# Four layers of a graph network in one kernel: in layer 0, squares, sums, norms and low halves issued later than what they need

## The chip, the cores and the metric

One Trainium2 chip, one of its cores. The metric is the device time of one execution in microseconds; the kernel before takes 1052.36 us (median of three runs, 1052.09 to 1052.92).

## The reference, cut to what matters

`x` is 8 x 2048 x 64, `adj` 2048 x 2048 (a 0/1 matrix with under 1% ones, rows divided by their sums). Four layers follow, each of the form `x = layernorm(x + f(x))`, the layer norm being over the 64 channels:

```python
# layer 0, K = 3, D = 16
w = einsum('nd,dkio->nkio', embedding, weight); b = embedding @ bias
As = [I, A, 2 A A - I]
out = einsum('bnki,nkio->bno', einsum('knm,bmc->bnkc', stack(As), x), w) + b
# layer 1: attention whose mask adj > 0.5 is nearly empty; in effect a mean over the rows, then elu
# layer 2: ((adj + I) @ (x W^T + b)) / rowsum;  layer 3: three steps of v = relu([v, adj v] W1 + b1) W2 + b2
```

## The kernel before, in words

**Layout.** Batch and channel are one axis of 512, cut into four chunks c of 128 columns (two batch entries). The 2048 nodes are 16 tiles of 128; four tiles make a part j. A pair (c, j) is a unit, u = 4c + j. The 0/1 matrix lies in SBUF in fp8, values in pairs of fp16 halves: a high half by ScalarE out of PSUM (`act_e1`, `act_e2`, `act_dx`: L1017, L1023, L1032) and a low half, the rest, by VectorE out of the same PSUM bank (`lo_half`, recorded as L1203). A bank is free for the next user when its low half is done.

**Layer 0.** Per unit a product P1 (A x) and a product P2 (A A x), each four quarters of 8 matmuls (`quarter`, L750), then per node tile t a round Z (L880): 36 matmuls against the 16 weight matrices, in two halves g of 18 matmuls, each into a pair of banks. For each half VectorE takes five of the eight results d with one operation each, multiplied with the embedding's column and added onto `X` or `Y` (L1203, the first `Y` L1195), ScalarE takes the other three (L1043, tiles `AT`), and GpSimd adds them up (`add`: a 128x384, two 128x128, two more onto X). ScalarE starts a half only after VectorE's last operation of it (`s_acc`), and after GpSimd's first operation of the add before (`s_ab`). TensorE may start half n when ScalarE has done half n - 2 (`s_za`).

There are 64 rounds, (u,t) or in one number 4u+t. Between rounds the order puts quarters of P1 (units 2, 3 of each chunk) and of P2 (the next unit, always bank 0), and in the first two units of chunks 0 to 2 after even rounds `dx` (L725, L726) and after odd rounds `t1` (L788, L789), of the next chunk. dx, t1 and the mean (L886) all use the one bank 1 (`pe_aux` waits until its last user is read out). GpSimd makes t1's low half (L1708).

**Layers 0 and 1 behind the rounds.** Each chunk c, when its 16 rounds are done, gets its layer norm: squares of each part (`sq`, ScalarE), their sum by VectorE (L1206, in the same step), a variance (`var`), a square root on ScalarE, a root refined in five small VectorE operations (`rs`, L1495 to L1499), and `apply` (L1505). Then `sum` over the parts (GpSimd, three 128x512 additions), `mean` (two fp32 matmuls against ones), `row_a`, `row_b` (VectorE and ScalarE, small), `addrow` onto X (GpSimd), squares and norm again (L = 1), and `split` into fp16 halves for layer 2 (ScalarE, GpSimd, and an addition by GpSimd). `scales` 0, 1, 2 are chains of small VectorE operations on scale factors, with two `hat` halves; they are needed in the tail.

**The order** is written by hand. `HEAD` (L84) is the list up to the first round, `middle_order` (L95) lays steps at places `(u, t)` of the rounds, and what falls behind the last round is given to `last_order` (L149), which writes the tail: products P(k) of layers 2 and 3 with evacuation E(k), and the rest beside them. Every engine walks the same list and takes its own part of each step (`tensor_steps`, `scalar_steps`, `vector_steps`, `gpsimd_steps`), in that order. The squares of layers 0 and 1 have one buffer, `SQ` in `T3`. In a round the list is:

```python
            order += [("Z", u, t), ("add", u, t)]
            order += after.pop((u, t), [])
            if c < 3 and j < 2:
                v = 4 * (c + 1) + 2 * j + t // 2
                order.append(("dx" if t % 2 == 0 else "t1", v))
```

`dve_xs` and `pool_xs` centre two tiles of x each and add the bias (`xs` 0 to 7); `bounds` ends with a GpSimd all-reduce over the partitions (L1741).

Of the kernel before, what the change touches and what calls it, by code (L numbers as in the profile page):

```python
# [14 lines left out]
NT = 16  # L15
# [65 lines left out]
def place(p, c, j):  # L81
# [9 lines left out]
        + [("xs", 0), ("xs", 1)]  # L91
        + pieces("P1", 2) + [("t1", 2), ("dx", 3), ("t1", 3), ("E1", 10), ("bounds",), ("xs", 2)]
# [3 lines left out]
def middle_order():  # L96

    after = {}
# [22 lines left out]
    order = []  # L121
    for k in range(5):
        at(k // 2, 1 + 2 * (k % 2), ("xs", 3 + k))
    at(2, 3, ("scales", 0))
    at(3, 1, ("scales", 1))
    at(3, 2, ("scales", 2))
    for u in range(16):
# [17 lines left out]
        order += after.pop((u, 4), [])  # L145
    return order, after


def last_order(after):  # L149
# [8 lines left out]
    for (u, t) in sorted(after):  # L158
        at(u - 16, *after[u, t])
    for c in range(NC):  # L160
        for j in range(4):
            at(4 * c + j + 3, ("W", c, j))
            at(4 * c + j + 4, ("sq", 2, c, j))
# [70 lines left out]
    between[55] = [("F", *x), ("sq", 3, *v), ("var3", *u)]  # L234
    on(56, ("root3", *u), ("rs3", *u), *outs(7, 5), ("F", *y), ("sq", 3, *x), ("sq", 3, *y), ("var3", *x), ("root3", *x),
# [38 lines left out]
def gnn_kernel(nc, x_in, at_in, a_in, embt_in, sm_in, bx_in, w0_in, a12_in, w0bb_in, out):  # L274
    ctx = ExitStack()
    with ctx:
# [147 lines left out]
        SQ = [T3[:, 512:1024]]  # L424
# [200 lines left out]
        SQN, SQPREV, VARN, RSN = {}, {}, {}, {}  # L625
# [5 lines left out]
        def number_norms():  # L631
            held = {}
            for x in MIDDLE + TAIL:
                if x[0] == "sq":
                    buf = 0 if x[1] < 2 else 2 * x[1] - 3 + len([y for y in SQN if y[0] == x[1]]) % 2
                    SQPREV[x[1:]] = held.get(buf)
                    SQN[x[1:]] = len(SQN)
                    held[buf] = x[1:]
                elif x[0] in ("var", "root3"):
# [6 lines left out]
        REDN = {x: n for n, x in enumerate(y for y in SQN if y[0] < 3 or order3(*y[1:]) > 12)}  # L646
# [14 lines left out]
        def sq_buf(L, c, j):  # L661
            return SQ[0] if L < 2 else SQC[2 * L - 4 + [y for y in SQN if y[0] == L].index((L, c, j)) % 2]
# [183 lines left out]
        def tensor_steps(e, steps):  # L846
            for step in steps:
# [9 lines left out]
                elif kind == "Z":  # L857
                    u, t = step[1:]
                    c, j = divmod(u, 4)
                    n4 = 4 * u + t  # L860
# [6 lines left out]
                    for g in range(2):  # L867
                        n = 2 * n4 + g
                        b0 = z_bank(n)
                        if n < 3:  # L870
                            for b in (b0, b0 + 1):
                                e.wait_ge(*z_first[b])
                        else:
                            e.wait_ge(s_za, 3 * (n - 2))
                        for i in range(9):
                            kd, part = divmod(i, 3)
                            zh, wh = ((0, 0), (0, 1), (1, 0))[part]
                            for q in range(2):
                                r = slice(64 * q, 64 * q + 64)
                                m = e.matmul(bank(b0 + q), halves[kd][zh][r, :], WZ[r, wh, kd, block(g)],  # L880
                                             start=(i == 0), stop=(i == 8))
                        m.then_inc(s_zp, 1)
# [158 lines left out]
        def scalar_steps(e, steps):  # L1041
# [3 lines left out]
            for step in steps:  # L1045
# [9 lines left out]
                elif kind == "scales" and step[1] == 0:  # L1055
# [5 lines left out]
                elif kind == "Z":  # L1061
                    u, t = step[1:]
# [4 lines left out]
                    for g in range(2):  # L1067
                        e.wait_ge(s_acc[0], 5 * n4 + (3, 5)[g])
                        e.wait_ge(s_acc[1], 5 * n4 + (2, 5)[g])
                        ps = zpair(2 * n4 + g)  # L1070
                        for d in range(DV, 8):
                            fn(grid(AT[:, 3 * g + d - DV, :]), ps[:, :, d, :], ACT.Copy,
                               scale=emb[:, it, 8 * g + d:8 * g + d + 1]).then_inc(s_za, 1)
# [291 lines left out]
        def vector_steps(e, steps, fc):  # L1365
# [31 lines left out]
            def scales_c():  # L1397
# [7 lines left out]
                for t in range(2):  # L1405
                    e.wait_ge(s_hh, 2 + t)
# [864 lines left out]
```

## Time and profile before

| | |
|---|---|
| median of 3 runs | 1052.36 us (1052.09 to 1052.92) |
| the profiled execution | 1052.66 us, its span 1050.9 us |
| TensorE matmul busy | 1023.4 us, 97% |
| TensorE clock granted | 0.996 of full |
| VectorE, ScalarE, GpSimd busy | 690.4, 453.4, 538.1 us |
| DMA | 45.66 MB, 43 GB/s on average, nearly all before 60 us and after 510 us |

The span runs from the first to the last instruction of the program. The head (loads, first products) lasts to about 103 us, the rounds of layer 0 from 110 to 531, the tail from there on. PE is TensorE, DVE VectorE, ACT ScalarE, POOL GpSimd. Idle times before an instruction stand in brackets behind it with who ended them.

### The profile page before, as it was taken

The page shows a single profiled execution, that of the slowest core. Times are in us where ns is not written, and L with a number is a line of the kernel's source. Part 1 is how long each engine was busy: PE and PEld are TensorE (multiplying, and loading weights), DVE is VectorE, ACT ScalarE, POOL GpSimd, SP SyncE. Part 2 cuts the span into 40 slices and gives each one's busy share as a digit, 9 for nine tenths or more (in the row PEclk, how much of TensorE's full clock was granted, in tenths as well). Part 3 has the DMA queues.
Part 4 walks back from the last instruction along what each step waited for, and adds up shares of the span by engine and source line. Part 5 has one row for each costly group of instructions (what it writes and reads, how often), then busy time and mean ns, then how long its engine had stood idle before and what let it go on. Part 6 is the DMA issues. An engine that isn't in the chain of part 4 may idle for free.

```text
span 1050.9 us, 18768 instructions
## 1 busy us (share of the span) xinstructions
PE 1023.4 (97%) x6922; PEld 490.9 (47%) x6922; DVE 690.4 (66%) x1728; ACT 453.4 (43%) x1097; POOL 538.1 (51%) x625
## 2 busy tenths in 40 slices
PE   7999999999999999999999999999999999999995
PEld 3445444434443444344345555555554545455553
DVE  3876565677547765775674778876546677767556
ACT  4632333333334343534423677557556622132632
POOL 0005486546456766775671757579764232223311
PEclk9999999999999999999999999999999999999998
DMA  9930000000000000000010121212112100000022
GB/s 365 400 128 1 2 1 2 1 2 1 1 1 2 1 1 2 1 1 2 1 41 1 41 81 41 81 41 80 53 69 81 41 1 1 3 2 21 22 61 61
DMA packets 14658, 45.66 MB, mean 43 GB/s; under 512 B 960, under 2 KB 9280, under 8 KB 10080
## 3 DMA queue, kind: packets, MB, share of 16 engines
q1 hardware_dynamic: 14560, 44.39, 11.4%
q8 instruction: 57, 0.93, 0.4%
q14 instruction: 41, 0.34, 0.1%
HBM read 40.19 MB, written 4.19 MB: 42 GB/s over the span
## 4 chain that ended last, share of the span: by engine, by line
PE 84%; DVE 9%; POOL 2%; ACT 2%; DMA 2%; issue 1%; SPq 0%; POOLq 0%; ACTq 0%; DVEq 0%
PE PS L750 34%; PE PS L880 21%; PE PS L924 18%; DMA BW<-at_in 2%; PE PS L735 2%; PE PS L737 2%; PE PS L736 2%; DVE BW L1200 1%; DVE T L1203 1%; DVE X L1203 1%; PE PS L744 1%; PE PS L742 1%; PE PS L743 1%; ACT T L1043 1%; PE PS L725 1%
## 5 line engine op out<-in xcount | busy, mean ns | idle before, releaser
L750 PE MATMUL PS<-BW,S 128*128 128x512 fp8e4 x1792 | 403.5, 379 | 4.3 <-POOL S L1708 1.9
L750 PEld LDWEIGHTS PS<-BW,S 128*128 128x128 f16 x1792 | 169.6, 98 | 211.0 <-issue 15.9
L1043 ACT ACTIVATE T<-PS,SM 128x128 f32<-128x128 f32 x384 | 112.5, 365 | 206.9 <-DVE X L1203 137.7
L880 PE MATMUL PS<-WZ,R 64*128 64x512 f16 x1536 | 198.5, 377 | 3.1 <-ACT T L1043 3.1
L1745 POOL TENSOR_TENSOR T<-T 128x128 f32<-128x128 f32 (+1 forms) x192 | 127.0, 662 | 124.9 <-ACT T L1043 114.4
L1203 DVE SCALAR_TENSOR_TENSOR X<-PS,SM,X 128x128 f32<-128x128 f32 x320 | 109.9, 344 | 38.7 <-PE PS L880 38.5
L880 PEld LDWEIGHTS PS<-WZ,R 64*128 64x128 f16 x1536 | 69.2, 94 | 106.8 <-issue 25.4
L924 PE MATMUL PS<-BW,S 128*128 128x512 fp8e4 x512 | 115.4, 379 | 0.4 <-issue 0.4
L1745 POOL TENSOR_TENSOR S<-R,S 128x512 f16<-128x512 f32 x48 | 57.5, 1210 | 94.2 <-ACT S L1043 94.2
L880 PE MATMUL PS<-WZ,T 64*128 64x512 f16 x768 | 103.8, 376 | 0.0
L1203 DVE SCALAR_TENSOR_TENSOR T<-PS,SM,T 128x128 f32<-128x128 f32 x256 | 88.0, 344 | 21.2 <-PE PS L880 21.2
L1745 POOL TENSOR_TENSOR T<-R,T 128x512 f16<-128x512 f32 x42 | 49.6, 1187 | 74.7 <-DVE T L1195 52.7
L1767 POOL TENSOR_TENSOR BW<-BW 128x512 fp8e4<-128x512 fp8e4 x64 | 75.6, 1208 | 0.0
L1043 ACT ACTIVATE R<-PS,cs 128x512 f32<-128x512 f32 x48 | 32.7, 681 | 98.7 <-PE PS L744 68.7
L924 PEld LDWEIGHTS PS<-BW,S 128*128 128x128 f16 x512 | 49.1, 98 | 55.9 <-issue 0.9
L924 PE MATMUL PS<-BW,T 128*128 128x512 fp8e4 x320 | 72.8, 379 | 0.0
L1745 POOL TENSOR_TENSOR X<-X,T 128x128 f32<-128x128 f32 x128 | 59.4, 464 | 10.0
L1043 ACT ACTIVATE WZ<-WZ,ra 128x2048 f16<-128x2048 f32 (+1 forms) x32 | 63.9, 1996 | 0.5
L1195 DVE TENSOR_SCALAR T<-R 128x512 f16<-128x512 f32 x48 | 31.5, 657 | 47.5 <-ACT R L1043 46.6
L802 PE MATMUL PS<-BW,S 128*128 128x512 fp8e4 x240 | 53.6, 386 | 6.0 <-DVE BW L1200 6.0
L735 PE MATMUL PS<-hat,T 128*128 128x128 f16 x320 | 56.8, 219 | 2.4 <-DVE T L1203 2.4
L880 PEld LDWEIGHTS PS<-WZ,T 64*128 64x128 f16 x768 | 37.4, 94 | 45.5
(215 smaller groups left out, 1476.9 us busy)
## 6 DMA issues: line engine op xcount, KB each, us to landing
WZ<-a_in SPq DMA_DIRECT2D x16, 1024.0 KB, 4.8
BW<-at_in SPq DMA_DIRECT2D x8, 1024.0 KB, 18.3
R<-at_in SPq DMA_DIRECT2D x7, 1024.0 KB, 13.7
out<-X SPq DMA_DIRECT2D x16, 256.0 KB, 2.3
X<-x_in SPq DMA_DIRECT2D x3, 1024.0 KB, 20.3
T<-w_in SPq DMA_DIRECT2D x1, 1536.0 KB, 16.0
R<-at_in SPq DMA_DIRECT2D x2, 512.0 KB, 5.2
SM<-sm_in SPq DMA_DIRECT2D x1, 520.5 KB, 18.3
```

What stands on the lines that cost most here:

```text
L735: e.matmul(ok, th, hat[:, 0, kind, :], start=True, stop=False)
L736: e.matmul(ok, tl, hat[:, 0, kind, :], start=False, stop=False)
L737: m = e.matmul(ok, th, hat[:, 1, kind, :], start=False, stop=True)
L750: m = e.matmul(o, stile(h, t, c), Bm[:, t, block(j)], start=(t == 0 and h == 0), stop=(last and t == NT - 1 and h == 1))
L802: e.matmul(bank(2 * c + j), stile(h, jt, c), Bm[:, jt, block(j)], start=(jt == 0 and h == 0), stop=False)
L880: m = e.matmul(bank(b0 + q), halves[kd][zh][r, :], WZ[r, wh, kd, block(g)], start=(i == 0), stop=(i == 8))
L924: m = e.matmul(o, half_of(n, what, h, q % 2)[:, t, :], b[:, 4 * (q % 2) + t, :], start=(s in (0, 1, 3) and q % 2 == 0 and t == 0 and h == ...
L1043: return e.activation(o, i, f, **kw)
L1195: return e.tensor_scalar(o, i, s1, None, o1)
L1203: return e.scalar_tensor_tensor(out=o, in0=a, scalar=s, in1=b, op0=f, op1=g)
L1745: return e.tensor_tensor(o, a, b, f)
L1767: e.tensor_tensor(o, a, b, f, saturate=False).then_inc(s_bt, 1)
```

## The change

Steps are laid at a round number g = 4u + t instead of (u, t), later and more spread than before. In chunks 0 to 2, with g the chunk's end: squares 2 or 3 rounds behind their unit's last round, their sum (a step of its own, `red`) a round behind the square; `var` at g+3, `rs` at g+4, one `apply` a round, `sum` at g+7, `mean` at g+9, `row_b` at g+10, `addrow` at g+11 to g+14, squares two rounds behind it, `var` at g+17, `apply` and `split` one a round from g+18. Chunk 3, whose steps mostly fall in the tail, has a denser list of its own. The low halves of P1's and P2's evacuations and of dx leave their step and go between VectorE's two halves of the next Z. Z is two steps (g = 0, 1). The first piece of `scales` is in two, the hat halves are steps of their own, and the long pieces go behind the first product of the tail. The squares get four buffers in the part of `BW` that later holds `BT`. In the head the second `xs` goes behind t1 2 and 3.

```diff
-        + [("xs", 0), ("xs", 1)]
-        + pieces("P1", 2) + [("t1", 2), ("dx", 3), ("t1", 3), ("E1", 10), ("bounds",), ("xs", 2)]
+        + [("xs", 0)]
+        + pieces("P1", 2) + [("t1", 2), ("dx", 3), ("t1", 3), ("xs", 1), ("E1", 10), ("bounds",), ("xs", 2)]
...
-    def at(u, t, *steps):
-        after.setdefault((u, t), []).extend(steps)
+    after, rest = {}, {}
+    def at(g, *steps):
+        (after if g < 64 else rest).setdefault(g if g < 64 else g - 64, []).extend(steps)
 
     for c in range(NC):
+        g = 16 * c
         for j in range(4):
-            at(4 * c + j + 1, 1, ("sq", 0, c, j))
-        u = 4 * c + 4
-        at(u, 2, ("var", 0, c))
-        at(u, 3, ("rs", 0, c), ("apply", 0, c, 0), ("apply", 0, c, 1))
-        at(u, 4, ("apply", 0, c, 2), ("apply", 0, c, 3), ("sum", c))
-        if c == 3:
-            u += 4
-        at(u + 1, 1, ("mean", c), ("row_a", c))
-        at(u + 1, 3, ("row_b", c))
-        for j in range(4):
-            at(u + 2, j, ("addrow", c, j))
-            at(u + 2, j + 1, ("sq", 1, c, j))
-        at(u + 3, 0, ("var", 1, c))
-        at(u + 3, 1, ("rs", 1, c), ("apply", 1, c, 0), ("split", c, 0))
-        for j in (1, 2, 3):
-            at(u + 3, j + 1, ("apply", 1, c, j), ("split", c, j))
+            late = (c, j) == (3, 3)
+            at(g + 4 * j + (5 if late else 6), ("sq", 0, c, j))
+            at(g + 4 * j + (6 if late else 7), ("red", 0, c, j))
+        g += 16
+        if c < 3:
+            at(g + 3, ("var", 0, c))
+            at(g + 4, ("rs", 0, c), ("apply", 0, c, 0))
+            for j in (1, 2, 3):
+                at(g + 4 + j, ("apply", 0, c, j))
+            at(g + 7, ("sum", c))
+            g += 9
+            at(g, ("mean", c), ("row_a", c))
+            at(g + 1, ("row_b", c))
+            for j in range(4):
+                at(g + 2 + j, ("addrow", c, j))
+                at(g + 4 + j, ("sq", 1, c, j))
+                at(g + 5 + j, ("red", 1, c, j))
+            at(g + 8, ("var", 1, c))
+            for j in range(4):
+                at(g + 9 + j, *[("rs", 1, c)][j:], ("apply", 1, c, j), ("split", c, j))
+        else:
+            at(g + 2, ("var", 0, c))
+            at(g + 3, ("rs", 0, c), ("apply", 0, c, 0), ("apply", 0, c, 1))
+            at(g + 4, ("apply", 0, c, 2), ("apply", 0, c, 3), ("sum", c))
+            at(g + 6, ("mean", c), ("row_a", c))
+            at(g + 7, ("row_b", c))
+            for j in range(4):
+                at(g + 7 + j // 3, ("addrow", c, j))
+                at(g + 8 + j // 3, ("sq", 1, c, j))
+                at(g + 9, ("red", 1, c, j))
+            at(g + 9, ("var", 1, c))
+            for j in range(4):
+                at(g + 10 + j // 2, *[("rs", 1, c)][j:], ("apply", 1, c, j), ("split", c, j))
     for k in range(5):
-        at(k // 2, 1 + 2 * (k % 2), ("xs", 3 + k))
-    at(2, 3, ("scales", 0))
-    at(3, 1, ("scales", 1))
-    at(3, 2, ("scales", 2))
+        at(2 * k + 1, ("xs", 3 + k))
+    at(9, ("scales", 0))
+    at(11, ("scales", 1))
+    at(13, ("scales", 2))
+    at(15, ("scales", 3))
+    at(65, ("scales", 4), ("scales", 5))
+    order, lo = [], []
...
                 order.append(beside.pop(0))
-            order += [("Z", u, t), ("add", u, t)]
-            order += after.pop((u, t), [])
+                if order[-1][0][0] == "E":
+                    lo.append(("lo", *order[-1]))
+            order += [("Z", u, t, 0), *lo, ("Z", u, t, 1), ("add", u, t)]
+            lo = []
+            order += after.pop(4 * u + t, [])
             if c < 3 and j < 2:
                 v = 4 * (c + 1) + 2 * j + t // 2
                 order.append(("dx" if t % 2 == 0 else "t1", v))
+                if t % 2 == 0:
+                    lo.append(("lo", *order[-1]))
...
-        SQ = [T3[:, 512:1024]]
+        SQ = [BW[:, NT * N + 2048 * k:NT * N + 2048 * k + 2048].bitcast(F32) for k in range(4)]
...
-                elif kind == "sq":
-                    L, c, j = step[1:]
-                    if L == 3 and summed_by_act(c, j):
-                        continue
+                elif kind == "red":
+                    L, c, j = step[1:]
                     o = st_part(L, c, j, 0)
                     e.wait_ge(s_sq, SQN[L, c, j] + 1)
                     red(e, o if L == 3 else o[:, 8 * j:8 * j + 8], grid(sq_buf(L, c, j)), ALU.add).then_inc(s_red, 1)
```

The tail's own lists get a `red` beside each `sq` whose sum VectorE makes, at the same place; the buffers of its squares stay.

## Rows read from the trace of the kernel before

**Rows 1.** The page, part 4: the chain that ended last, by engine.
```profile
PE 84%; DVE 9%; POOL 2%; ACT 2%; DMA 2%; issue 1%; SPq 0%; POOLq 0%; ACTq 0%; DVEq 0%
```

**Rows 2.** Timeline of TensorE, round (6,3): start us, us, engine, line, operation.
```profile
306.62 0.82 PE L880 MATMUL PS<-WZ,R 64*128 64x512 f16 x6
...
310.61 1.90 PE L750 MATMUL PS<-BW,S 128*128 128x512 fp8e4 x8
```

**Rows 3.** Timeline of TensorE: the longer rounds, and a mean without a wait.
```profile
214.88 0.82 PE L880 MATMUL PS<-WZ,R 64*128 64x512 f16 x6
...
221.20 1.90 PE L750 MATMUL PS<-BW,S 128*128 128x512 fp8e4 x8 [1.80 <-DVE R L1203]
...
257.83 0.82 PE L880 MATMUL PS<-WZ,R 64*128 64x512 f16 x6
...
263.97 0.23 PE L788 MATMUL PS<-i,T 128*128 128x128 f16 x1 [1.03 <-DVE ROW L1206]
...
264.43 3.62 PE L750 MATMUL PS<-BW,S 128*128 128x512 fp8e4 x16
...
368.25 0.82 PE L880 MATMUL PS<-WZ,R 64*128 64x512 f16 x6
...
374.99 0.23 PE L788 MATMUL PS<-i,T 128*128 128x128 f16 x1 [1.62 <-DVE ROW L1206]
...
418.93 0.82 PE L880 MATMUL PS<-WZ,R 64*128 64x512 f16 x6
...
421.98 0.82 PE L880 MATMUL PS<-WZ,R 64*128 64x512 f16 x6 [0.94 <-ACT T L1043]
...
424.03 1.90 PE L750 MATMUL PS<-BW,S 128*128 128x512 fp8e4 x8
...
470.73 1.13 PE L886 MATMUL PS<-SM,ones 128*128 128x512 f32 x2
471.70 1.89 PE L750 MATMUL PS<-BW,S 128*128 128x512 fp8e4 x8
```

**Rows 4.** The chain in order of time: one product of the tail.
```profile
547.03 6.91 PE PS L750 x32
```

**Rows 5.** Timelines of TensorE, GpSimd and ScalarE around the head's end.
```profile
103.13 7.08 PE L750 MATMUL PS<-BW,S 128*128 128x512 fp8e4 x32 [1.93 <-POOL S L1708]
...
123.98 1.46 PE L880 MATMUL PS<-WZ,R 64*128 64x512 f16 x12
...
117.83 1.03 POOL L1717 TENSOR_TENSOR X<-X,hat 128x512 f32<-128x512 f32 x1 [6.93 <-issue]
...
123.54 1.66 ACT L1043 ACTIVATE T<-PS,SM 128x128 f32<-128x128 f32 x6 [6.45 <-POOL T L1745]
```

**Rows 6.** Timelines of VectorE, TensorE: Z, a low half, who waits.
```profile
116.41 0.82 PE L880 MATMUL PS<-WZ,R 64*128 64x512 f16 x6
...
118.64 0.35 DVE L1203 SCALAR_TENSOR_TENSOR X<-PS,SM,X 128x128 f32<-128x128 f32 x1 [0.82 <-PE PS L880]
...
308.78 0.35 DVE L1203 SCALAR_TENSOR_TENSOR X<-PS,SM,X 128x128 f32<-128x128 f32 x1 [0.73 <-PE PS L880]
...
309.82 0.34 DVE L1203 SCALAR_TENSOR_TENSOR X<-PS,SM,X 128x128 f32<-128x128 f32 x1
...
334.32 0.69 DVE L1203 SCALAR_TENSOR_TENSOR R<-PS,R 128x512 f16<-128x512 f32 x1 [1.42 <-ACT R L1023]
334.93 0.34 DVE L1203 SCALAR_TENSOR_TENSOR X<-PS,SM,X 128x128 f32<-128x128 f32 x1
...
335.07 1.25 PE L750 MATMUL PS<-BW,S 128*128 128x512 fp8e4 x5
```

**Rows 7.** Applies (ns min/median/max), one root with its apply.
```profile
L1505 DVE TENSOR_TENSOR X<-X,T x28: 682/904/1758, 248.5 to 546.1; 128x512 f32<-128x512 f32 x28
...
324.78 0.34 DVE L1495 RECIPROCAL T<-T 128x32 f32<-128x32 f32 x1
...
327.07 0.69 DVE L1505 TENSOR_TENSOR X<-X,T 128x512 f32<-128x512 f32 x1
```

More of the change, by code:

```diff
@@ L144, in middle_order @@
                 order.append(("dx" if t % 2 == 0 else "t1", v))
-        order += after.pop((u, 4), [])
-    return order, after
+                if t % 2 == 0:
+                    lo.append(("lo", *order[-1]))
+    return order, rest
 def last_order(after):
@@ L156, in at @@
         late.setdefault(k, []).extend(steps)
-    for (u, t) in sorted(after):
-        at(u - 16, *after[u, t])
+    for k in sorted(after):
+        at(k, *after[k])
     for c in range(NC):
@@ L661, in sq_buf @@
         def sq_buf(L, c, j):
-            return SQ[0] if L < 2 else SQC[2 * L - 4 + [y for y in SQN if y[0] == L].index((L, c, j)) % 2]
+            return (SQ + SQC)[SQBUF[L, c, j]]
         def st_part(L, c, j, k, m=1):
@@ L866, in tensor_steps @@
                               [U2[:, u % 3, h, 128 * t:128 * t + 128] for h in range(2)])
[L867 to L882, printed above, removed]
+                    n = 2 * (4 * u + t) + g
+                    b0 = z_bank(n)
+                    if n < 3:
+                        for b in (b0, b0 + 1):
+                            e.wait_ge(*z_first[b])
+                    else:
+                        e.wait_ge(s_za, 3 * (n - 2))
+                    for i in range(9):
+                        kd, part = divmod(i, 3)
+                        zh, wh = ((0, 0), (0, 1), (1, 0))[part]
+                        for q in range(2):
+                            r = slice(64 * q, 64 * q + 64)
+                            m = e.matmul(bank(b0 + q), halves[kd][zh][r, :], WZ[r, wh, kd, block(g)],
+                                         start=(i == 0), stop=(i == 8))
+                    m.then_inc(s_zp, 1)
                 elif kind == "mean":
@@ L1054, in scalar_steps @@
                     act_e2(e, step[1])
-                elif kind == "scales" and step[1] == 0:
+                elif kind == "scales" and step[1] == 1:
                     e.wait_ge(s_xc, NT)
@@ L1066, in scalar_steps @@
                         e.wait_ge(s_ab, n4)
[L1067 to L1073, printed above, removed]
+                    e.wait_ge(s_acc[0], 5 * n4 + (3, 5)[g])
+                    e.wait_ge(s_acc[1], 5 * n4 + (2, 5)[g])
+                    ps = zpair(2 * n4 + g)
+                    for d in range(DV, 8):
+                        fn(grid(AT[:, 3 * g + d - DV, :]), ps[:, :, d, :], ACT.Copy,
+                           scale=emb[:, it, 8 * g + d:8 * g + d + 1]).then_inc(s_za, 1)
                 elif kind == "sq":
@@ L1404, in scales_c @@
                 e.wait_ge(s_sc, 1)
-                for t in range(2):
-                    e.wait_ge(s_hh, 2 + t)
-                    stt(e, hat[:, 1, t:4:2, :], BD[:, t::2, :], cs[:, cRho64 + t:cRho64 + t + 1], hat[:, 0, t:4:2, :],
-                        ALU.mult, ALU.subtract).then_inc(s_hl, 1)
             for step in steps:
                 kind = step[0]
-                if kind == "E1":
-                    dve_e1(e, step[1])
+                if kind == "lo" and step[1] == "E1":
+                    dve_e1(e, step[2])
+                elif kind == "lo" and step[1] == "E2":
+                    dve_e2(e, step[2])
+                elif kind == "lo" and step[1] == "dx":
+                    dve_dx(e, step[2])
+                elif kind == "lo":
+                    e.wait_ge(s_zh, 1)
+                    lo_half(e, T[:, 0, 1, block(0)], bank(product_bank(0)), T[:, 0, 0, block(0)], s_zl)
@@ L1524, in vector_steps @@
                     ts(e, ROW[:, 0, :], ROW[:, 0, :], LAM, None, ALU.mult).then_inc(s_row, 1)
-                elif kind == "E":
+                elif kind == "E" and step[1] > 0:
                     k = step[1]
```

83 lines of the change are left out of this document (42 added, 41 removed).

## The prediction

> **What bounds it now.** The chain that ended last [rows 1] is 84% TensorE, so a part of the kernel off TensorE counts only where it makes TensorE wait. The change touches layer 0 (about 103 to 531 us) and the first products of layer 1 behind it. A busy share says little there: matmuls are drawn 0.38 us long while they start every 0.11 or 0.22 us, so short waits vanish in it. I read the timeline of TensorE, start to start; (u,t) is round t of unit u, number 4u+t. A quiet round (36 matmuls of Z) takes 3.99 us from its first matmul to the first of what follows [rows 2]: 306.62 to 310.61. Every other round is held against that.
>
> The rounds that take longer [rows 3] are these. Round (3,3): 214.88 to 221.20 is 6.32, so 2.33 lost; VectorE was in the scale steps 1 and 2, Z's second half came late and then the product waited for bank 0's low half (1.80 idle). Round (5,1): 257.83 to the t1 at 263.97 is 6.14; the mean's two fp32 matmuls cost 0.97 where nobody waits (470.73 to 471.70), so 1.18 lost, TensorE wanting bank 1 while VectorE had still to reduce the mean. Round (9,1): 368.25 to 374.99, 1.78 lost in the same way. Rounds (7,1), (11,1), (15,1): 418.93 to 424.03 is 5.10, 1.11 lost in each of the three; the wait is for ScalarE's copies (421.98), which stood behind a VectorE that was held by the one buffer of squares and by addrow. Together 2.33 + 1.18 + 1.78 + 3 x 1.11 = 8.6 us, plus some 0.2 in two small waits: **8.8 us** is all that TensorE waits between its first round and the layer's end.
>
> **What the change removes.** The two long scale steps go to the tail's second step, and the hat halves to rounds 13 and 15: the 2.33 go. About 5 us of small VectorE operations land beside the tail's products, where a stage has 32 matmuls of product, 6.91 us, at the least [rows 4], and its low half is wanted two products later: cost nothing; without that cover it would be their 5 us. The means go to rounds 25, 41 and 57, where no dx or t1 follows for bank 1: 1.18 + 1.78 go (the mean's own 0.97 stays). Squares come two rounds behind addrow, with four buffers, and sums a round behind the squares: the 3 x 1.11 go. Nothing is added in instruction count; the squares only change address, and the writer of BT gets to those 8 KB a row late in the tail. For chunk 3, sums, mean and splits come 3 or 4 tail stages later; product 12 wants them at stage 12 and they are issued at 10 and 11, so nothing again. No DMA moves; GpSimd's queue keeps its operations, with sum 4 rounds later.
>
> **The head.** TensorE stands 1.93 us before 103.13 for GpSimd's t1 [rows 5]. With the second xs behind t1 it would come about 2 us sooner. But GpSimd's work to the first add is the same sum in another order: after it comes the all-reduce, and xs 2 begins at 117.83 as before. ScalarE's copies of round 1 wait for the first add and start at 123.54 and are six in 1.66; half of them are done 0.9 later, and the second half of round 2 (the second six of the twelve matmuls at 123.98, so about 124.63) needs it. TensorE can start it at 124.48 at the earliest. Gain 0.15, not 2.
>
> **What the change adds: low halves behind Z's first half.** A low half frees a PSUM bank: bank 0 for the next product, bank 1 for the t1 behind dx. Until now VectorE did it ahead of Z, in idle time. Now it stands behind the five operations of Z's first half. In a quiet round [rows 2, 6] these start at 308.78, 2.16 after the round's start, the fifth at 309.82, so the low half at 310.08, 3.46 in. From a low half's start to the matmul that waits for it: 334.32 to 335.07 is 0.75 (this low half is late already, ahead of (8,0)). So TensorE may go on at 4.20, and could at 3.99: **a stall of 0.21**. In chunk 0 the first operation comes at 2.23 (116.41 to 118.64): 0.28. Where dx's and a product's low halves stand together, the second starts 0.61 later (334.32 to 334.93), that is allowed at 4.81; t1 starts at 4.20 and gives over after 0.46 (263.97 to 264.43): another 0.15.
>
> Counting from the order: ten rounds have a product's low half alone before bank 0 is wanted (chunk 0: three; rounds (6,3), (7,3), (10,3), (11,3), (12,3), (13,3), (14,3); at (6,1) the mean covers it): 3 x 0.28 + 7 x 0.21 = 2.3. Dx alone: (4,1), (8,1), (9,1), 0.6 (the one at (0,1) is swallowed by the wait at 124.5). Both: three in chunk 0, five later: 3 x 0.43 + 5 x 0.36 = 3.1. Sum **6.0 us lost**, in 21 small waits.
>
> **What else makes a low half late.** VectorE is free from about 5.4 us into a round to 2.16 into the next: 2.6 us in short rounds (5.82), 3.0 in those with dx or t1 (6.27). A root (rs, five operations) and one apply took 2.9 (324.78 to 327.07, and 0.61 of the apply's 0.69) [rows 7]. That fits after round 34, is 0.3 over after round 50 (a low half follows), and round 36 has rs and two applies, 0.9 over; with the waits behind them about **1.1 us**. The bounds: nothing, if the pieces are the quick ones; and 5.3 us if every apply is the slowest of its row (1.76) and every root the slow one (2.28): 1.0 + 2.8 + 1.5.
>
> That spread has a cause in the rows: the same apply takes 0.68 to 1.76 [rows 7], and it is the longer ones that stand beside GpSimd's additions; the change puts splits (two GpSimd operations a round) and applies in the same rounds. The Trainium skill says so too (SBUF — State Buffer, on the shared port pair): a VectorE operation with two SBUF inputs and a GpSimd operation exclude each other, the later fully blocked. By that rule the upper bound is the one to fear; by the rows' median of 0.90 it is the middle one. The trace agrees with the rule in kind, its share here is open.
>
> **Sum.** 8.8 + 0.15 - 6.0 - 1.1 = 1.9 us faster. The profiled execution took 1052.66 (span 1050.9), 0.3 above the median of 1052.36; so 1050.8 for it, and **1050.4** as a median. About 0.2% (2.1 us) is what a measurement here can tell from none, and this lies just within it.
>
> **Rivals.**
> 1. *The low halves cost TensorE next to nothing*: bank 0 and 1 come free in time, as they do wherever TensorE arrives late. Then 8.8 + 0.15 - 1.1 = 7.9, 1044.5. For it: 0.2 us on a 4 us round is thin, and half of it gone gives 1047.5. Against: each of the three terms (2.16, 1.30, 0.75) is a plain difference of two rows of a quiet stretch. Chance 0.17.
> 2. *Slower*: VectorE is late with low halves in many rounds, since applies and roots now run beside splits and additions and take their slow lengths. Place: rounds 34 to 37 and 50 to 53, then each low half behind them. Price: 5.3 us by the upper bound above, 8.95 - 6.0 - 5.3 = -2.4, 1054.7. It decides (slower by over 0.2%) from 5.1 us of lateness on. Chance 0.08.
> 3. *The change does not do all that it says*: a removed wait comes back elsewhere, for instance Z's second half still waits for ScalarE in three rounds (3.3 us), since GpSimd's queue has sum, t1 and splits in the way: 1053.7. For it: copies wait for GpSimd's first operation of the add before (6.45 us idle at 123.54). Against: from that operation's usual time to the moment at which it would hurt are 5 us, and sum is 3.8. Chance 0.15.
>
> **Numbers.** Forecast 0.60, its own range 1048.7 to 1052.3. It lies on the bound of faster (1050.26), so it splits: 0.25 faster, 0.35 within. Rival 1 is faster, rival 3 is within but for 0.02, rival 2 is slower. Faster 0.43, same 0.48, slower 0.09. The range goes down half way to rival 1, since a stall of 0.1 in place of 0.2 is the nearest error, and up beyond the forecast toward rival 3: 1046.5 to 1053.2.
>
> **What the profile would show.** TensorE's rounds (3,3), (5,1), (7,1), (9,1), (11,1), (15,1) at 3.99 (4.96 with a mean), or the step is wrong. Quiet rounds with a low half at 4.20 in place of 3.99, and waits of products and t1 on VectorE's low halves: some 21 of 0.2 to 0.4 us. The page's span near 1049. The second half of round 2 still at about 124.5 with the wait on ScalarE. No new wait of TensorE behind layer 0. If the low halves' waits are absent the forecast is wrong by up to 6 us, if there are waits over 0.5 us behind rounds 34 to 53, rival 2 is at work.

## The result and the profile after

The changed kernel takes 1056.1 us (median of 9 runs, 1054.34 to 1057.28) against 1052.8 of the kernel before beside it (9 runs, 1052.09 to 1053.77): ratio 1.003 with the interval 1.002 to 1.0041, so it is slower by 3.3 us. Its profiled execution took 1056.91, that of before 1052.66, so the comparison of the traces has 4.25 us to explain. The prediction was 1050.4 (range 1046.5 to 1053.2): wrong in sign, and outside its range.

The page of the changed kernel: span, engines, and the chain of work that ended last by engine:

```profile
span 1055.1 us, 18890 instructions
...
PE 1027.2 (97%) x6922; PEld 492.1 (47%) x6922; DVE 691.8 (66%) x1728; ACT 452.7 (43%) x1097; POOL 533.6 (51%) x625
...
PE 76%; DVE 14%; issue 3%; ACT 3%; DMA 2%; POOL 2%; SPq 0%; ACTq 0%; DVEq 0%; POOLq 0%
```

TensorE's share of the chain fell from 84% [rows 1] to 76% and VectorE's rose from 9% to 14%: TensorE is waiting for VectorE in more places. Where, the view of TensorE's waits says, here for 100 to 540 us, which is layer 0 (line, releaser: us in total, times, longest):

```profile
PE PS L820 <- DVE R L1232: 3.1, 6, 2.0
PE PS L910 <- ACT T L1073: 1.7, 1, 1.7
PE PS L782 <- DVE R L1232: 1.2, 3, 0.8
...
```

The same view of the changed kernel for 540 to 1040 us:

```profile
PE PS L767 <- DVE R L1232: 1.6, 2, 1.0
PE PS L757 <- DVE X L1232: 1.0, 1, 1.0
...
```

Before, the second stretch had 0.8 us of waits, at 916 and 1036 us, none of them in the tail's first 120 us. As in the prediction, the waits are better read start to start. The two traces laid side by side, the 4.25 us come out as:

| where | us |
|---|---|
| first round starts at 107.75 instead of 110.14 | -2.39 |
| its low half, and round 2, which waits 1.83 in its middle | +2.10 |
| the six long rounds [rows 3] are at 3.99 (the means 0.95 more) | -8.8 |
| low halves behind Z's first half | +6.0 |
| rounds 35, 37 and 51 longer than that (0.14, 1.84, 0.64) | +2.6 |
| TensorE at its lower clock in round 37 | +1.6 |
| three waits in the tail | +3.05 |
| sum (trace: last round +1.12, from there on +3.1) | 4.2 |

**A low half costs what was worked out.** Timeline of TensorE of the changed kernel in round (6,3), the quiet round of [rows 2]:

```profile
306.19 0.82 PE L910 MATMUL PS<-WZ,R 64*128 64x512 f16 x6
...
310.39 0.82 PE L782 MATMUL PS<-BW,S 128*128 128x512 fp8e4 x3
```

And of VectorE beside it, the first operation of Z's first half and the low half behind the fifth:

```profile
308.35 0.35 DVE L1232 SCALAR_TENSOR_TENSOR X<-PS,SM,X 128x128 f32<-128x128 f32 x1 [2.92 <-PE PS L910]
...
309.65 0.68 DVE L1232 SCALAR_TENSOR_TENSOR R<-PS,R 128x512 f16<-128x512 f32 x1
```

306.19 to 310.39 is 4.20 where before had 3.99. The same 0.21 stands in every such round of chunks 1 to 3, 0.27 or 0.28 in chunk 0, and 0.15 more where dx's and a product's low halves stand together.

**Round 37 waits far longer, and then TensorE runs at half clock.** Timeline of VectorE of the changed kernel:

```profile
366.92 1.33 DVE L1537 TENSOR_TENSOR X<-X,T 128x512 f32<-128x512 f32 x1
368.17 0.34 DVE L1527 RECIPROCAL T<-T 128x32 f32<-128x32 f32 x1
368.55 0.77 DVE L1528 TENSOR_TENSOR T<-T 128x32 f32<-128x32 f32 x1
369.35 0.92 DVE L1529 TENSOR_TENSOR T<-T 128x32 f32<-128x32 f32 x1
...
370.51 0.33 DVE L1531 TENSOR_TENSOR T<-T 128x32 f32<-128x32 f32 x1
370.88 0.99 DVE L1537 TENSOR_TENSOR X<-X,T 128x512 f32<-128x512 f32 x1
...
373.09 0.67 DVE L1232 SCALAR_TENSOR_TENSOR R<-PS,R 128x512 f16<-128x512 f32 x1
```

And of TensorE, first matmul of the t1 that waits for it, and the product behind:

```profile
373.82 0.23 PE L820 MATMUL PS<-i,T 128*128 128x128 f16 x1 [1.98 <-DVE R L1232]
...
374.28 3.43 PE L782 MATMUL PS<-BW,S 128*128 128x512 fp8e4 x8
```

From 366.92 to 371.87 VectorE has two applies and a root between two rounds of Z, 4.95 us where such a round leaves it 3.0, so 1.95 too much. L1528 and L1529, 0.19 in a quiet root, take 0.77 and 0.92 beside GpSimd's low half of t1 (367.66 to 369.26) and its additions for Z (from 369.23); the applies take 1.33, beside the split's addition, and 0.99. So Z's first half and the low half behind it are late, and the t1 waits till 373.82. The eight matmuls at 374.28 then take 3.43 instead of 1.90. The view of that window gives busy time of each engine and, third from the end, the granted clock:

```profile
374.00:377.70 3.70, 3.70 (x18) 1.35 (x17) 3.04 (x8) 2.16 (x6) 2.76 (x3) 0.56 0.00 0
```

That is about half speed (1.2 GHz in place of 2.4) after 1.98 us of standing still.

**The tail.** A stage is one product of the tail with the steps beside it; place 64 + k in the list is stage k. Timeline of GpSimd of the changed kernel, 611 to 638 us:

```profile
611.17 1.16 POOL L1777 TENSOR_TENSOR S<-X,S 128x512 f16<-128x512 f32 x1 [16.67 <-ACT S L1073]
...
628.53 3.20 POOL L1799 TENSOR_TENSOR BW<-BW 128x512 fp8e4<-128x512 fp8e4 x3
631.69 2.48 POOL L1777 TENSOR_TENSOR X<-X,bc 128x512 f32<-128x512 f32 x2
634.13 4.09 POOL L1799 TENSOR_TENSOR BW<-BW 128x512 fp8e4<-128x512 fp8e4 x3
```

VectorE of the same stretch:

```profile
629.21 0.34 DVE L1527 RECIPROCAL T<-T 128x32 f32<-128x32 f32 x1
629.59 1.14 DVE L1528 TENSOR_TENSOR T<-T 128x32 f32<-128x32 f32 x1
630.76 1.02 DVE L1529 TENSOR_TENSOR T<-T 128x32 f32<-128x32 f32 x1
631.82 1.18 DVE L1225 TENSOR_SCALAR T<-T 128x32 f32<-128x32 f32 x1
633.03 1.20 DVE L1531 TENSOR_TENSOR T<-T 128x32 f32<-128x32 f32 x1
634.26 3.02 DVE L1537 TENSOR_TENSOR X<-X,T 128x512 f32<-128x512 f32 x2
```

And the three waits of TensorE behind it:

```profile
641.69 0.23 PE L767 MATMUL PS<-hat,T 128*128 128x128 f16 x1 [0.58 <-DVE R L1232]
...
651.30 0.23 PE L757 MATMUL PS<-dg,S 128*128 128x128 f16 x1 [0.96 <-DVE X L1232]
...
652.93 0.23 PE L767 MATMUL PS<-hat,T 128*128 128x128 f16 x1 [1.01 <-DVE R L1232]
```

GpSimd stands 16.67 us for ScalarE's part of chunk 3's split, which the change put several stages later, and pieces of BT (L1799) stand behind that split in its queue. Six pieces had run ahead of it, at 588.13. When it goes on, the next nine come in threes, at 617.08, 628.53 and 634.13, and the last two groups, with two additions (631.69) between them, meet a root and two applies on VectorE, those of layer 2's norm of chunk 1 in stage 12. In the kernel before GpSimd was done with the same pieces at 619.9 and had nothing to do until 632.4 (timeline of GpSimd):

```profile
616.69 3.21 POOL L1767 TENSOR_TENSOR BW<-BW 128x512 fp8e4<-128x512 fp8e4 x3
632.42 2.72 POOL L1745 TENSOR_TENSOR S<-R,S 128x512 f16<-128x512 f32 x2 [12.53 <-ACT S L1043]
```

And VectorE of the kernel before, the same root and applies:

```profile
623.85 0.19 DVE L1496 TENSOR_TENSOR T<-T 128x32 f32<-128x32 f32 x1
624.07 0.19 DVE L1497 TENSOR_TENSOR T<-T 128x32 f32<-128x32 f32 x1
624.30 0.18 DVE L1196 TENSOR_SCALAR T<-T 128x32 f32<-128x32 f32 x1
624.52 0.19 DVE L1499 TENSOR_TENSOR T<-T 128x32 f32<-128x32 f32 x1
624.74 1.29 DVE L1505 TENSOR_TENSOR X<-X,T 128x512 f32<-128x512 f32 x2
```

The four small ones took 0.75 together, they take 4.54 now; the two applies 1.29, now 3.02. TensorE waits three times for what stands behind them: 0.74, 1.13 and 1.18 longer than before, start to start.

### The profile page after: what moved, and what is told of

Its sections match the earlier page's. It is cut to its first block, busy times and chain, and to the rows that moved or that the text cites. A ratio compares the mean times of both kernels' runs of the same rounds, so it can differ in the third digit from the quotient of the medians.

```text
span 1055.1 us, 18890 instructions
## 1 busy us (share of the span) xinstructions
PE 1027.2 (97%) x6922; PEld 492.1 (47%) x6922; DVE 691.8 (66%) x1728; ACT 452.7 (43%) x1097; POOL 533.6 (51%) x625
## 4 chain that ended last, share of the span: by engine, by line
PE 76%; DVE 14%; issue 3%; ACT 3%; DMA 2%; POOL 2%; SPq 0%; ACTq 0%; DVEq 0%; POOLq 0%
PE PS L782 29%; PE PS L910 19%; PE PS L954 18%; DVE R L1232 2%; DVE X L1232 2%; DVE T L1232 2%; DMA BW<-at_in 2%; PE PS L767 1%; PE PS L769 1%; PE PS L768 1%; DVE BW L1229 1%; ACT WZ L1073 1%; DVE S L1232 1%; DVE X L1537 1%; PE PS L776 1%
## 5 line engine op out<-in xcount | busy, mean ns | idle before, releaser
L1777 POOL TENSOR_TENSOR T<-T 128x128 f32<-128x128 f32 (+1 forms) x192 | 123.8, 645 | 136.1 <-ACT T L1073 125.9
L1799 POOL TENSOR_TENSOR BW<-BW 128x512 fp8e4<-128x512 fp8e4 x64 | 75.7, 1210 | 0.0
```

The source lines that it names most:

```text
L1777: return e.tensor_tensor(o, a, b, f)
L1799: e.tensor_tensor(o, a, b, f, saturate=False).then_inc(s_bt, 1)
```

## The experiments

Theory A after the result: three separate causes, each local. The low halves behind Z's first half (6 us and the lateness on top); chunk 3's new places in the tail (3 us); and against them the waits removed (8.8). Theory B: VectorE and GpSimd are simply more often side by side, so that undoing one part moves the stall and gains little. "Low half early" below means that the two places that gather low halves put them back into the order at once:

```diff
-                    lo.append(("lo", *order[-1]))
+                    order.append(("lo", *order[-1]))
```

**Low halves early, the rest as changed** (the diff above).

> The changed kernel with one part undone: the low halves stand again where they stood, right behind their high half's step, ahead of Z on VectorE. In the trace of the changed kernel TensorE waits 7.5 us for low halves in layer 0 behind round 2 (6 us of it in waits of 0.20 to 0.35, the rest behind late applies), 1.2 us more in the second of two low halves, and after its longest wait (1.98 us, at 371.8) its clock stands at half speed for 3.4 us, 1.6 us lost. Theory A (the low halves' place costs all of this): 1056.1 - 10 = about 1046. Theory B (VectorE is simply late behind roots and applies, wherever the low halves stand): only the quiet waits go, 1056.1 - 6.5 = about 1049.5. Theory C (tail alone is to blame): 1056 or more. The tail's 3 us of waits at 641 to 653 stay in all of them.

Measured: 1050.34 us (10 runs, 1048.67 to 1052.27), ratio 0.998 (0.9971 to 0.999). 5.8 us under the changed kernel; the profiled execution (1048.67, the fastest) has no small wait left in layer 0, but rounds 35, 37 and 51 are still 0.35, 1.4 and 0.86 long and the three waits of the tail stand. So low halves late cost about what the steps said, and the lateness of round 37 is there without them. (Trace against trace the two kernels are 8.2 apart, in part because this one's profiled execution has no stretch at the lower clock in layer 0. Eight of its ten runs show a granted clock of 0.993 to 0.995 and take 1050.09 or more, the two at 0.997 took 1048.67 and 1048.80.) That round 51 waits has another link than the root: ScalarE's turn. Timeline of ScalarE of this kernel:

```profile
451.12 0.63 ACT L1073 ACTIVATE S<-X 128x512 f16<-128x512 f32 x1 [1.77 <-DVE X L1537]
...
452.18 0.58 ACT L1053 ACTIVATE R<-PS 128x512 f16<-128x512 f32 x1
```

And VectorE's low half behind it:

```profile
452.79 0.69 DVE L1232 SCALAR_TENSOR_TENSOR R<-PS,R 128x512 f16<-128x512 f32 x1 [1.76 <-ACT R L1053]
```

ScalarE's high half of the product (452.18) stands behind a split that waits for VectorE's apply, and VectorE's low half waits for the high half.

**Chunk 3's steps at their old places** (stages 0, 5, 6 and 7; its squares and sums of layer 0 one or two rounds sooner with them), the rest as changed. Cut, and `*applies` stands for the four applies, which the kernel writes out:

```diff
-            at(g + 2, ("var", 0, c))
-            at(g + 3, ("rs", 0, c), ("apply", 0, c, 0), ("apply", 0, c, 1))
-            at(g + 4, ("apply", 0, c, 2), ("apply", 0, c, 3), ("sum", c))
-            at(g + 6, ("mean", c), ("row_a", c))
-            at(g + 7, ("row_b", c))
+            at(64, ("var", 0, c), ("rs", 0, c), *applies, ("sum", c))
+            at(69, ("mean", c), ("row_a", c), ("row_b", c))
```

and its addrow, squares and splits at places 70 and 71, which are stages 6 and 7.

> The changed kernel with another part undone: chunk 3's norms, sums, mean and splits at their old stages of the tail (0, 5, 6, 7 in place of 2 to 11). Theory A (the splits of chunk 3 at stages 10 and 11 hold GpSimd's queue, its BT pieces come in a bunch afterwards and stretch VectorE's root and applies, and TensorE waits 0.74 + 1.13 + 1.18 us for W and D): the three waits at 641 to 653 go, 1056.1 - 3.1 = about 1053. Theory B (the tail's waits come from something else that was moved, the scale steps or chunk 2): they stay, 1056.

Measured: 1052.68 (10 runs), ratio 1.0004 (0.9994 to 1.0014): 3.4 under the changed kernel. The three waits in the tail are gone and all of layer 0's stand: A's number.

**Both together.**

> Both parts undone: low halves early, chunk 3 at its old stages. What is left of the change are the later squares, sums, norms and means of chunks 0 to 2, four buffers, the scale steps moved, the head's xs swapped. If the two losses are independent and the waits that the change removes in layer 0 (8.8 us in the trace of before) stay away: 1052.8 - 9 = about 1043.5, 13 under the changed kernel. If removing them was worth nothing by itself (waits come back elsewhere): about 1050 to 1053.

Measured: 1045.84 (1045.24 to 1046.38), ratio 0.9939 (0.9923 to 0.9956). This is 6.6 faster than the kernel before beside it (1052.44). The two parts add, 5.8 and 3.4, and 1.1 more; these four runs all show a granted clock of 0.996 or 0.997, those of the two kernels with one part undone go down to 0.993, so the 1.1 can be the clock's, which is not shown. The time is 2.3 short of A's 1043.5, and the trace has that: rounds 35, 37 and 51 are 0.35, 1.41 and 0.86 too long, which A had charged to the low halves.

**The kernel before with the low halves late alone** (Z as two steps, the low half between them, and what goes with it: four buffers, split scale steps, the head's swap; squares, means, norms where they were).

> The kernel before in the order of its steps, with the low halves late alone (and the four buffers, the split scale steps and the head's swap, which should be worth under 0.5 us). In quiet rounds it costs 0.20 to 0.43 us in 23 places, 6 us; before, VectorE was also late into many rounds (its first operation of Z 2.5 to 6.5 us behind the round's start in some fifteen of them in the trace, in place of 2.16), and every lateness in a round with a low half is now a wait of TensorE. Theory A: 1052.8 + 6 + 3 to 8 of lateness = 1062 to 1067, more than the whole loss of the change. Theory B (low halves cost nothing by themselves, the new layout of norms is what costs): 1053.

Measured: 1059.27 (1058.95 to 1061.28), ratio 1.0072 (1.0055 to 1.0089), 6.8 slower than before. In the trace the last round of layer 0 starts at 533.86 instead of 527.49, 6.4 later: 1.3 in round (3,3), where TensorE now waits 3.02, the rest in the quiet rounds, some of whose 0.21 vanish in a wait that stood there already. That is under the 1062 to 1067 expected: the old stalls and the low halves overlap more than they add.

**Where the last 2.3 us are: root and applies spread.** From "both" on: the root alone in a round, an apply in each of the next four, then sum, mean, its row and addrow a round later than in the change; the squares behind them stay. In the second norm too the root is alone, and the applies and splits come one or two rounds later. Cut:

```diff
-            at(g + 4, ("rs", 0, c), ("apply", 0, c, 0))
-            for j in (1, 2, 3):
-                at(g + 4 + j, ("apply", 0, c, j))
-            at(g + 7, ("sum", c))
+            at(g + 4, ("rs", 0, c))
...
+                at(g + 5 + j, ("apply", 0, c, j))
+            at(g + 8, ("sum", c))
+            at(g + 10, ("mean", c), ("row_a", c))
+            at(g + 11, ("row_b", c))
...
-                at(g + 9 + j, *[("rs", 1, c)][j:], ("apply", 1, c, j), ("split", c, j))
...
+            at(g + 18, ("rs", 1, c))
...
+                at(g + 19 + j + (j > 0 and c < 2), ("apply", 1, c, j), ("split", c, j))
```

> The kernel with low halves early and chunk 3 at its old stages (1045.84), and in chunks 0 to 2 the roots in rounds without an apply beside them and no more than two applies in a round. In the trace of both_undone TensorE still waits 0.35 + 1.41 + 0.86 us in rounds 35, 37 and 51: at 35 and 51 ScalarE's high half stands behind a split that waits for VectorE's apply, at 37 VectorE itself is late (one root of 3.6 us between two applies). Theory A (place decides): these 2.6 go, about 1043.2. Theory B (VectorE and GpSimd collide wherever they meet): the waits turn up in other rounds, 1045 to 1046.

Measured: 1045.0 (1044.89 to 1045.24), ratio 0.9927 (0.991 to 0.9944). Rounds 35, 37 and 51 are clean, but 0.74 came back at round 42 (the mean waits for GpSimd's sum, now a round later) and 1.0 at 603.8 in the tail. So 2.6 us went and 1.7 came: it is B's number.

**BT's pieces earlier in GpSimd's queue**, low halves early, chunk 3 as changed:

```diff
-        at(8 + i // 3, ("bt", i))
+        at(i // 3 if i < 24 else 14 + (i - 24) // 3, ("bt", i))
```

> The kernel with low halves early and chunk 3 at its new late stages (low_early, 1050.34), with GpSimd's BT pieces moved alone: 24 of the 64 at stages 0 to 7, none at 8 to 13, the rest from 14 on. Theory A (the tail's three waits of 3 us come from the collision of VectorE's root and applies with BT pieces that were held up behind the splits in GpSimd's queue; five small operations of that root took 5.0 us at 629 to 634 in place of 1.3): the waits go or shrink to under 1 us, 1047.5. Theory B (ScalarE's later copies and splits at stages 10 and 11 delay the low halves, the norm of chunk 0 and all behind it): the waits stay, 1050.

Measured: 1046.07 (1045.8 to 1047.14), ratio 0.9941 (0.9924 to 0.9957): 4.3 under the same kernel without the move, and the tail's three waits are gone. The root at 620 is quick again. VectorE of this kernel:

```profile
620.40 0.34 DVE L1527 RECIPROCAL T<-T 128x32 f32<-128x32 f32 x1
620.78 0.19 DVE L1528 TENSOR_TENSOR T<-T 128x32 f32<-128x32 f32 x1
...
621.67 1.29 DVE L1537 TENSOR_TENSOR X<-X,T 128x512 f32<-128x512 f32 x2
```

The split is as late as in the changed kernel; only what stands in GpSimd's queue beside the root has changed. So it is not chunk 3's lateness as such but the pieces that it holds back. The gain is 4.3 where A had expected 3: in the traces the tail is 2.7 shorter (from the last round's start to TensorE's last matmul), and 2.7 is also what the runs say when that kernel's two at a granted clock of 0.997 (1048.67, 1048.80) are taken. The rest goes with the clock of its other eight; these four show 0.995 to 0.997.

**The changed kernel itself with BT's pieces moved** (the same diff, low halves late).

> The changed kernel itself (1056.1) with the BT pieces moved alone; low halves late, chunk 3 at the new stages. Moving them took 4.3 us off low_early. Theory A (the tail's loss is its own and adds to that of the low halves): 1056.1 - 4.3 = 1051.8, so that the change would have come out at the kernel before or a little under. Theory B (part of the 4.3 came from elsewhere, through states of single executions): 1053 (3.05 us of waits in the trace).

Measured: 1051.94 (1051.02 to 1053.48), ratio 0.9996 (0.9986 to 1.0005): A's 1051.8. Here too part of the 4.2 is the clock: at a granted clock of 0.997 the changed kernel took 1054.34 (one run), this one 1051.02 to 1051.86 (three), and the tail's waits in the trace are 3.05. Layer 0's waits are those of the changed kernel, 1.98 before round 37's t1 among them.

**The scale steps back at rounds 11, 13 and 14**, on "both":

```diff
-    at(9, ("scales", 0))
-    at(11, ("scales", 1))
-    at(13, ("scales", 2))
-    at(15, ("scales", 3))
-    at(65, ("scales", 4), ("scales", 5))
+    at(11, ("scales", 0), ("scales", 1))
+    at(13, ("scales", 4))
+    at(14, ("scales", 5), ("scales", 2), ("scales", 3))
```

> both_undone (1045.84) with the scale steps back at rounds 11, 13 and 14. Theory A (as predicted: the scale steps alone cost 2.33 us, the wait at the end of round 15): 1048.2. Theory B (that wait had needed the single buffer and the old squares too): 1046.

Measured: 1046.99 (1046.73 to 1047.15), ratio 0.9946 (0.9929 to 0.9963), 1.15 over "both". Round 15 waits 0.42, not the 2.33 of [rows 3]: with squares and sums out of the way the same long pieces almost fit. (Its trace starts the first round at 108.33, "both" at 107.35, but round 2 takes half of that back, and the kernels with this same head start it anywhere from 107.33 to 108.33: that is how much the head differs from one execution to the next.) So the 2.33 was the price of the pieces together with what stood beside them, and at most half of it is their own.

**Two buffers of squares in place of four** (`% 2` for `% 4`, on "both").

> both_undone (1045.84) with two buffers of squares in turn, in place of four. Squares and sums are a round apart in the new order, at most two are open at once but for the stages of chunk 3. Theory A (the order brings the gain, the buffers beyond the second nothing): 1045.8 within 0.5. Theory B (ScalarE is held at the third square and its copies come late): 1047 to 1049.

Measured: 1046.05 (1045.55 to 1046.45), ratio 0.9939: no difference. Behind the new spacing the third and fourth buffer do nothing. Whether a second is needed wasn't tried.

**The head's second xs at its old place**, on "both".

> both_undone (1045.84) with the head's second xs back ahead of t1 2 and 3. Theory A (as predicted: GpSimd's all-reduce and the first add set when round 2 goes on, the head's order is worth 0.15 to 0.3): 1046.1, with TensorE's wait of 1.9 back at 103 and the one of 1.8 in round 2 gone. Theory B: the 2.4 us that the rounds start sooner are kept, 1048.

Measured: 1046.09 (1045.83 to 1046.6), ratio 0.9941. TensorE stands 1.9 us before 103 again and the wait in round 2 is gone. The medians are 0.25 us apart and the ranges overlap, so the swap is worth little, as worked out (0.15), and not 2; how little these runs don't tell. The traces don't either: round 3 starts 0.87 sooner in "both" than here, but against the kernel before the swapped head gave anything from 1.27 sooner to 0.15 later (one kernel left out whose clock fell there).

**Spread, with BT's pieces moved** (the two diffs above, chunk 3 at its old places).

> spread (1045.0) with the BT pieces moved as in bt_moved. In spread's trace TensorE waits 1.0 us once in the tail, at 603.8, for a low half of VectorE behind applies that take 1.2 to 1.8 us beside BT pieces; and 0.74 in round 42. Theory A (the two cures add): the wait at 603.8 goes, 1044. Theory B (the tail had slack left and the wait moves on): 1045.

Measured: 1051.5 (1050.38 to 1052.37, 11 runs), ratio 0.9989 (0.998 to 0.9998): a miss by 7 us, 6.5 slower than "spread". The same collision in another place. Timeline of GpSimd of this kernel:

```profile
542.11 9.52 POOL L1796 TENSOR_TENSOR BW<-BW 128x512 fp8e4<-128x512 fp8e4 x9
```

VectorE beside it, those of the longest scale steps and the low half behind:

```profile
543.26 1.02 DVE L1229 SCALAR_TENSOR_TENSOR cs<-cs 128x1 f32<-128x1 f32 x1
544.31 1.02 DVE L1406 TENSOR_TENSOR cs<-cs 128x1 f32<-128x1 f32 x1
...
546.31 2.19 DVE L1221 TENSOR_SCALAR cs<-ones,cs 128x4 f32<-128x4 f32 x2
...
550.65 1.02 DVE L1222 TENSOR_SCALAR ra<-ra,cs 128x16 f32<-128x16 f32 x1
...
552.20 0.69 DVE L1229 SCALAR_TENSOR_TENSOR T<-PS,T 128x512 f16<-128x512 f32 x1
```

And TensorE, which waits for it:

```profile
552.99 0.27 PE L764 MATMUL PS<-hat,T 128*128 128x128 f16 x1 [5.05 <-issue]
...
554.22 7.78 PE L779 MATMUL PS<-BW,S 128*128 128x512 fp8e4 x32
```

Nine pieces run at 542 to 552, beside the scale steps on columns of one element: single operations of 1.02 where the short ones take 0.15. With chunk 3's norm at stage 0 in front of them, the low half at 552.20 is late and TensorE waits 5.05 us, then runs its next product in 7.78 where such a row is 7.08 long [rows 5] (granted clock 0.56 from 553 to 556 us).

**The same with the mean and its row at g+11.**

> spread_bt with the mean and both row steps at g+11 in place of g+10 and g+11: at g+10 of chunk 1 TensorE waits 0.74 us for GpSimd's sum. Theory A: that wait goes, 0.7 us under spread_bt. Theory B (VectorE, which now waits for ScalarE's exponential between row_a and row_b, is late with the next low half): same or up to 1 us over.

Measured: 1050.66 (1050.35 to 1051.95, 11 runs), ratio 0.9985 (0.9976 to 0.9994). The wait at round 42 is gone, 0.8 under the run above; the 5.1 us at 550 stand. (In its trace the granted clock is 0.51 from 548.5 to 555.5 and the product behind takes 8.97; the runs of both kernels go from 0.992 to 0.995, so the 0.8 between the medians is not the clock's.)

**Chunk 3's norm at stage 0 and moved pieces, without the spread** ("both" and BT moved): is it that meeting, or the spread?

> both_undone (1045.84: low halves early, chunk 3 at its old stages, nothing spread) with the BT pieces moved. Theory A (old stages of chunk 3 and early BT pieces do not go together): the wait of 5 us near 550 and the half clock behind it appear here too, 1051 to 1052. Theory B (the spread list is what does not go with early BT pieces): 1045 to 1046.

Measured: 1049.07 (1048.4 to 1051.72, 8 runs), ratio 0.997 (0.9959 to 0.998): 3.2 over "both", with waits of 1.1 at 548.8 and 1.7 at 607.7, between the two theories. So the meeting of chunk 3's old places with the pieces is worth about half of the 6.5, and the rest comes with the spread. The traces say how: with the spread chunk 3's root starts at 534.84 in place of 532.97, and nine pieces in a row stand beside the scale steps in place of six (from 540.25), so that three more operations there take 0.8 to 1.0 us. Which of the spread's moves does it isn't taken apart.

**All parts where they don't meet:** low halves early, chunk 3 at the change's places, root and applies spread, mean at g+11, BT's pieces moved.

> bt_moved (1046.07: low halves early, chunk 3 at its new stages, BT pieces moved) with the roots and applies of chunks 0 to 2 spread and the mean at g+11. In spread_mean layer 0 was left with round 2's wait alone; bt_moved has none in the tail's first part. Theory A (what went wrong in spread_bt is the meeting of BT pieces at stages 0 and 1 with chunk 3's four applies and the long scale steps, which only the old list has there): 1046.07 - 2.6 = about 1043.5. Theory B (the spread list's chunk 2, one round later, or the scale steps alone meet the early BT pieces): a wait of 1 to 5 us near 550, 1046 to 1051.

Measured: 1043.23 (1042.47 to 1043.88, 5 runs), ratio 0.9914 (0.99 to 0.9927): 9.45 us under the kernel before beside it (1052.68) and the fastest of all. TensorE's waits of 100 to 540 us in this kernel:

```profile
PE PS L908 <- ACT T L1071: 1.0, 1, 1.0
```

That is round 2 of the head, and the last wait that layer 0 has.

## Why the prediction was wrong, step by step

- **"What the change removes", 8.8 us: right.** All six rounds are at their floor, in the changed kernel and in every kernel built from it. One term was read too narrowly: the 2.33 of round (3,3) belongs to the scale steps and the squares together.
- **"The head", 0.15: right in kind, small and not 2** (0.29 in the trace, 0.25 in the run that undid it, both less than the head differs between executions).
- **"What the change adds", 6.0: right**, to the row (4.20 for 3.99). Undoing it gave 5.8; adding it alone cost 6.8.
- **"For chunk 3 ... so nothing again": the step that failed.** It checked when product 12 wants the result, which is in time, but not what else stands in the queue that the step was moved in. GpSimd's queue runs in order: a split that comes later holds back the pieces of BT behind it, and these then meet a root and applies of layer 2's norm. Price in the trace 3.05 us; 3.4 by putting chunk 3 back, 4.3 by putting the pieces first, of which the tail is 2.7 and the clock the rest. The text had named the writer of BT as late and drew no price from it.
- **"What else makes a low half late", 1.1: too small**, 2.6 measured, of which 1.84 at round 37 alone (6.04 against 4.20). The counts of operations were right (a root and two applies), the durations not: the root had been taken at 2.29, the length of one in which two small operations were already stretched, and it took 2.71, the two applies 2.24 together. The upper bound of the sum, 5.3, held; that of a root, 2.28, did not, and in the tail one took 5.05. At round 51 (0.64) the place was right and the link another: not VectorE's own time but ScalarE's high half behind a split.
- **The clock: not in the prediction at all.** 1.6 us of the profiled execution. It is no fixed part of the price, see below: of the nine runs the one with a granted clock of 0.997 took 1054.34, three at 0.996 1054.56 to 1055.93, five at 0.994 and 0.995 1056.1 to 1057.28. So the median has some of it too, and even the run with the highest clock is slower than every run of before beside it (1053.77 at most).

In sum: the -8.8, the -0.3 and the +6.0 came as forecast; +1.1 came as +2.6, and +3.05 and +1.6 came where nothing was forecast. With the forecast's other terms the tail alone turns 1.9 faster into 1.2 slower.

Of the rivals, the second came nearest (1054.7, given 0.08): VectorE late because applies and roots run beside splits. Its place was half right, round 37 but also the tail, where what VectorE meets is not the splits but mostly the pieces behind them. The nearness of its number is in part luck: of its 5.3 us of lateness 2.6 came, and the tail and the clock made up the rest. The first was ruled out by every quiet round. The third was ruled out too: no removed wait came back. The list of what would show the prediction wrong had the decisive line ("No new wait of TensorE behind layer 0"), but no case of the forecast had been given to it, and so the range ended at 1053.2.

## What to carry to other kernels

When a step moves later, ask of each in-order queue that it is in what stands behind it there, and what those held-back operations will meet when they are let go: a deadline that is kept proves only half. Work that frees a PSUM bank goes first on its engine; five short operations in front of it cost 0.2 to 0.4 us in each of 21 rounds, which is invisible in a busy share and comes to 6 us. And a change of several parts with gains and losses is worth taking apart: here one was worth 9 us, hidden by two others that cost 6 and 3.

## What the runs showed of the hardware

**Short VectorE operations beside GpSimd's.** TENSOR_TENSOR and SCALAR_TENSOR_TENSOR on 32 columns or on one, 0.15 to 0.19 us alone, take up to 1.0 or 1.2 beside GpSimd's operations of 1.06 to 1.37 us each (the rows' lengths by their counts): at most about one such operation more, and some of them less (0.33 and 0.77 in round 37). RECIPROCAL stays at 0.34 in both, and the operations on PSUM at 0.34. The Trainium skill (SBUF — State Buffer, section "SBUF: two separate sides") has it that the SBUF port pair which the two engines share is an exclusive lock for the whole instruction; the trace agrees, the wait is about what is left of one GpSimd operation. It also lists VectorE operations with two SBUF inputs or in a 2-port mode as the ones concerned. The TENSOR_SCALAR at 631.82, with one SBUF tensor in, took 1.18 instead of 0.18, so one input was enough here; whether it ran in such a mode no view shows.

**The clock after a wait.** TensorE ran at half clock for 3.4 us behind the 1.98 us wait of the changed kernel. The identical wait in the kernel with chunk 3 at its old places had no such thing. TensorE of that kernel:

```profile
372.86 0.23 PE L818 MATMUL PS<-i,T 128*128 128x128 f16 x1 [1.99 <-DVE R L1230]
...
373.32 1.89 PE L780 MATMUL PS<-BW,S 128*128 128x512 fp8e4 x8
```

1.89 for the product that took 3.43. So did the changed kernel with BT's pieces moved (1.98 waited, then 1.89), and even the 3.02 us wait in the kernel with the low halves late alone (1.90). In the kernel with the spread and BT's pieces moved, a wait of 1.99 us in round 2 was followed by the same fall: granted clock 0.54 from 125.3 to 128.7, and 1.6 us lost; the thirteen other kernels with this head wait 1.0 to 1.7 there and show none. In the 5.05 us wait above the clock fell while TensorE still stood. A wait of 2 us may thus be followed by a fall that costs 1.6 us more, in some executions and not in others; what decides it these runs don't show.
